# A sandwich layer on one core: norm, transposes and q, k, v products of blocks 1 and 2 made one block ahead, in two homes

## The reference

```python
h = layernorm(x); xc = silu(causal_conv4(h))                 # along the tokens
q, k = l2norm(h @ Wq), l2norm(h @ Wk)                        # per head, 16 heads of 16
v = layernorm(h @ Wv)                                        # per head
i, gamma = sigmoid(xc @ Wig + big), sigmoid(xc @ Wg + bg)
mem[t] = gamma[t] * mem[t-1] + i[t] * k[t] * v[t]            # a scan along the tokens
out = groupnorm(layernorm(mem) * q) * sigmoid(xc @ Wog + bog)
h = x0 + out @ Wo;  y = h + (silu(ln(h) @ Wgate) * (ln(h) @ Wval)) @ Wout    # FF = 1024
```

## Time and profile before

| | us |
|---|---|
| median of 3 runs (569.54 to 570.79) | 569.62 |
| profiled execution, whole | 570.92 |
| its span, first to last instruction | 569.2 |
| TensorE busy, products of `BUSY` among it | 529.4 |
| products of `BUSY` (L887), 254 records | 33.1 |
| VectorE busy | 387.9 |
| ScalarE busy | 267.5 |
| GpSimd busy | 108.1 |

### The profile page before, as it was taken

How to read it: one execution, slowest core, us unless ns; L and a number is a source line. 1 busy time by engine, 2 the same in 40 slices (tenths; PEclk the granted TensorE clock), 3 DMA queues, 4 the chain that set the end, 5 groups by cost and what they waited for, 6 DMA issues and landing times.

```text
span 569.2 us, 8506 instructions
## 1 busy us (share of the span) xinstructions
PE 529.4 (93%) x2646; PEld 424.9 (75%) x2646; DVE 387.9 (68%) x1165; ACT 267.5 (47%) x489; POOL 108.1 (19%) x133
## 2 busy tenths in 40 slices
PE   7989889997799999999999997999996899999983
PEld 6568655876567777876687885888875799999872
DVE  5998847788756889853976962515567666767547
ACT  4943755154654243576414337111344456666605
POOL 1500041000033320004041000050014024444500
PEclk9999899999799999999999999999999999999997
DMA  8951000010200020120010001020139224444284
GB/s 282 419 200 38 2 0 0 1 37 1 74 1 0 30 85 1 37 74 1 1 47 28 31 9 37 1 75 1 38 85 284 86 78 131 124 130 132 79 294 158
DMA packets 29631, 44.56 MB, mean 78 GB/s; under 512 B 3164, under 2 KB 24284, under 8 KB 29244
## 3 DMA queue, kind: packets, MB, share of 16 engines
q1 hardware_dynamic: 24595, 33.07, 18.3%
q0 software_dynamic: 3408, 9.38, 4.5%
q10 hardware_dynamic: 1584, 1.57, 0.9%
HBM read 27.67 MB, written 16.34 MB: 77 GB/s over the span
## 4 chain that ended last, share of the span: by engine, by line
PE 72%; DVE 14%; ACT 6%; DMA 4%; issue 2%; SPq 0%; POOL 0%; DVEq 0%; POOLq 0%; ACTq 0%
PE psum L868 15%; PE psum L827 12%; PE psum L828 12%; PE psum L829 12%; PE psum L909 6%; PE psum L933 3%; DMA RDNR<-rdn 2%; PE psum L887 2%; PE psum L968 2%; PE psum L837 2%; PE psum L929 2%; PE psum L1047 1%; PE psum L1064 1%; DVE XC L1403 1%; DMA YF<-y_routed 1%
## 5 line engine op out<-in xcount | busy, mean ns | idle before, releaser
L729 ACT ACTIVATE SM<-psum 128x512 f32<-128x512 f32 (+1 forms) x56 | 33.1, 594 | 118.5 <-PE psum L829 89.0
L1578 DVE TENSOR_TENSOR SM<-SM,psum 128x512 f32<-128x512 f32 (+1 forms) x56 | 38.3, 683 | 54.3 <-ACT SM L729 50.3
L593 POOL DMA_INDIRECT x_dispatched<-XN,dest x32 | 33.2, 1038 | 155.9 <-DVE XN L1646 147.4
L868 PE MATMUL psum<-WOU,SM 128*128 128x256 f32 x256 | 60.4, 380 | 0.0
L868 PEld LDWEIGHTS psum<-WOU,SM 128*128 128x128 f32 x256 | 48.0, 189 | 10.1 <-issue 1.9
L584 POOL TENSOR_TENSOR QKV<-QKV,hvec 128x256 f32<-128x256 f32 x16 | 12.3, 771 | 206.3 <-ACT IG L665 178.0
L602 POOL DMA_INDIRECT y_routed<-GO,g_dest x39 | 37.6, 965 | 68.1 <-ACT GO L799 67.8
L909 PE MATMUL psum<-WQKV,HT 128*128 128x512 f32 (+1 forms) x128 | 46.2, 509 | 3.6 <-ACT QKV L658 1.9
L868 PE MATMUL psum<-SDN,SM 128*128 128x256 f32 (+1 forms) x192 | 44.6, 381 | 0.0
L909 PEld LDWEIGHTS psum<-WQKV,HT 128*128 128x128 f32 x128 | 24.8, 199 | 23.8 <-issue 18.9
L868 PEld LDWEIGHTS psum<-SDN,SM 128*128 128x128 f32 (+1 forms) x192 | 35.8, 189 | 6.6 <-issue 1.3
(11 more groups left out here) (325 smaller groups left out, 1295.6 us busy)
## 6 DMA issues: line engine op xcount, KB each, us to landing
XG<-x_dispatched SPq DMA_DIRECT2D x39, 130.0 KB
YF<-y_routed SPq DMA_DIRECT2D x8, 512.0 KB, 7.1
RUPR<-rup SPq DMA_DIRECT2D x1, 2816.0 KB
X<-x SPq DMA_DIRECT2D x4, 512.0 KB, 6.4
x_after_attention<-X SPq DMA_DIRECT2D x4, 512.0 KB, 2.8
...
```

The lines of the kernel that those rows point to most:

```text
L593: nc.gpsimd.indirect_dma_start(XD[:, :], bass.IndirectOffsetOnAxis(dest[:, i, old + j:old + j + 1], 0), XN[:, j, :], None).then_inc(dispat ...
L729: nc.scalar.activation(SM[0:rows, g % 3, 0:tb], p_pair(n)[0][0:rows, 0:tb], ACT.Silu).then_inc(silu_ready, 1)
L868: last = nc.tensor.matmul(p_down[:, j // 2, (j % 2) * D:(j % 2 + 1) * D], SM[0:rows, g % 3, j * P:(j + 1) * P], weight[0:rows, m, :], star ...
L1578: nc.vector.tensor_tensor(SM[0:rows, g % 3, 0:tb], SM[0:rows, g % 3, 0:tb], value_rows(n, rows)[:, 0:tb], ALU.mult).then_inc(hid_ready, 1)
```

## The change

- A second home `QKV1` stands beside `QKV`; block b uses home b % 2 (`qkv(b)`). It lies where the squares of block 0 lay; these move into room that is free then.
- Block 1's rows are not fetched: `ln0` reads them from `X[:, 1]`, which is loaded anyway, and whose load is issued right behind the gate weights, ahead of Wo, Wgate, Wval and Wout.
- `q` is now only products and copy; squares, sums and GpSimd's scaling are a step of their own, `sq`.
- `ht`, `q` of block 1 stand behind `mt` of block 0 on TensorE, `ht`, `q` of block 2 among the last steps of block 1, ahead of its `h2` (`_rows`). Both blocks use banks 2 to 5 for q, k, v in turns of two (`q_banks`) and `p_down` for the transposes (`ht_banks`). New waits on TensorE keep these banks apart: `ht` of block 1 waits for block 0's scan, that of block 2 for `mlp_read`; `og` and `wo` of block 0 wait until the copies of block 1's q, k, v are through.
- On VectorE, `ln0` of block 1 moves from behind block 0's `norm` 1 to ahead of its first `sq`; `split` 1 from behind `h2` 1 to ahead of `sq` 2. The root of the first half of block 0's k and v is a Sqrt on ScalarE and a reciprocal in place of eight steps on VectorE.
- `BUSY` falls from 127 products to 42; none stands any more ahead of `og`, `ht` 2, `xt` 0 and the second `h2`.
- The tables of `PLACE` and `FIRST` are new for all blocks.

```diff
+    early = [s for s in rows[1] if s[0] == "q"]
+    at = rows[0].index(("ht", 2, 0)) + 1
+    rows[0][at:at] = early
...
 FIRST = {
     "pe": """
-        ht:0 q:0 q:1 q:2 q:3 g:0 g:1 g:2 ut:0a ut:0b mt:0a mt:0b og:0a og:0b wo:0a wo:0b ht:+0 h2:0a h2:0b q:+0 q:+1
-        q:+2 mup:0 q:+3 mup:1""",
+        ht:0 q:0 q:1 q:2 q:3 g:0 g:1 g:2 ut:0a ut:0b mt:0a mt:0b ht:+0 q:+0 q:+1 q:+2 q:+3 og:0a og:0b wo:0a wo:0b
+        h2:0a h2:0b mup:0 mup:1""",
...
 BUSY = {
-    ("ht", 0, 0, 0): 26, ("ut", 0, 0, 0): 9, ("mt", 0, 0, 1): 10, ("og", 0, 0, 0): 46, ("og", 0, 0, 1): 16, ("h2", 0, 0, 0): 8,
-    ("ht", 2, 0, 0): 4, ("xt", 0, 0, 0): 6, ("h2", 1, 0, 0): 2,
+    ("ht", 0, 0, 0): 18, ("ut", 0, 0, 0): 10, ("mt", 0, 0, 0): 8, ("h2", 0, 0, 0): 6,
 }
...
         def q_banks(b, m):
+            if b in (1, 2):
+                return psum[:, 2 + 2 * (m % 2):4 + 2 * (m % 2), :]
             return psum[:, 2 * m:2 * m + 2, :] if b == 0 else p_main
...
+        def qkv(b):
+            return (QKV0, QKV1)[b % 2]
+        def normed_from(b, j):
+            return X[:, 1, j, :] if b == 1 else qkv(b)[:, j, 0:D]
+        def ht_banks(b):
+            return p_down if b in (1, 2) else p_main
...
             sp.dma_start(GW[:, :, D:2 * D], rows(wog)).then_inc(w_in["gw"], 16)
+            load_x(1)
             sp.dma_start(WO[:, :, :], rows(wo)).then_inc(w_in["wo"], 16)
...
             load_x(0)
-            load_x(1)
...
# ScalarE
-                if stage == "fetch" and b > 0:
-                    act.wait_ge(affined, prior)
+                if stage == "fetch" and b > 1:
+                    act.wait_ge(affined, PSTART[b - 1])
...
+                if stage == "rs" and u == 0 and m == 1:
+                    both = slice(0, 2 * len(mine) * HEADS)
+                    act.wait_ge(var_done["rs"], 1)
+                    nc.scalar.activation(rs[:, both], va[:, both], ACT.Sqrt).then_inc(root_ready["rs"], 1)
...
# TensorE
+                    if stage == "og":
+                        pe.wait_ge(qkv_copied, START[2] - 1)
...
                 if (stage, m) == ("ht", 0):
                     if b == 1:
-                        pe.wait_ge(normed, prior)
-                    if b > 1:
+                        pe.wait_ge(mem_ready, C * prior)
+                    if b == 2:
+                        pe.wait_ge(mlp_read, 1)
+                    if b > 2:
                         pe.wait_ge(hr_ready, prior)
-                    to_features(p_main, lambda j: QKV[:, j, 0:D], nj, hn_ready, old).then_inc(ht_psum, 1)
+                    to_features(ht_banks(b), lambda j: qkv(b)[:, j, 0:D], nj, hn_ready, old).then_inc(ht_psum, 1)
...
                 if stage == "wo":
                     if b == 0:
                         pe.wait_ge(w_in["wo"], 16)
+                        pe.wait_ge(qkv_copied, START[2])
...
# VectorE
+                    elif u == 0:
+                        dve.wait_ge(root_ready["rs"], 1)
+                        pairs = y.rearrange("p (j h) -> p j h", j=len(mine))
+                        nc.vector.reciprocal(rr[:, t0:t1, HEADS:], pairs).then_inc(rr_ready, 1)
```

122 lines of the change are left out of this document (75 added, 47 removed), and 48 rows, old and new, of the table PLACE.

## The result

| | before | after |
|---|---|---|
| median of 4 runs each on one chip | 570.20 (569.54 to 571.14) | 563.84 (562.82 to 564.56) |
| profiled execution, its span | 570.92, 569.2 | 562.82, 561.0 |
| mean granted clock of TensorE | 0.983 | 0.971 |

What follows compares the result with a forecast made beforehand. TensorE's work was taken to bound the kernel outside two holes where it waits for VectorE. Terms -7.5 and -6.6 gave -14.1 on the profiled 570.9, so 556.8, median 555.5; range 549 to 564 for 8 in 10.

Steps and rivals of the forecast that it cites:

- q products in the holes cost nothing: TensorE's waits in block 0's attention and between blocks 0 and 1: q products moved there are free at full clock.
- `norm` 1 ends at 57.9: Block 0's start on VectorE: net 2.9 us later, so `norm` 1 ends at 57.9 instead of 55.0.
- 14.4 us from `norm` 1 to H2L: Block 0: H2L 14.4 us after `norm` 1 instead of 18.1, ending at 72.3, when the first `mup` starts.
- 17.8 from there to `ut`: From H2L at 72.3, 10.1 us to the root and 7.7 to `u`'s end; block 1's `ut` at 90.1.
- first term: Gain at block 1's `ut` from its q products in the first hole: -7.5 us, bounds -10.3 and -3.
- After the hole 7.95 are gone: Behind the second hole, three of block 2's q products leave TensorE's path: 2.79 + 2.58 + 2.58 = 7.95 us.
- 1.3 for ScalarE's copies: Second hole: block 2's last q copy and XN stand ahead of `ln2` on ScalarE, costing 1.3 us.
- Second term: Gain from block 2's q products in the second hole: -7.95 + 1.3 = -6.6 us, bounds -10 and -2.
- The rest 0: From block 2's `ut` on, nearly the same order and path as before: 0 us, within -1 and +2.
- The clock as it is: The sum leaves the number of TensorE clock falls on the path unchanged; each costs about 1.6 us.
- one of the holes is not free: Rival: queued copies delay `h2` and `xt`, or the start is 4 us later; one term shrinks to a third; 560.5, chance 0.12.
- The signs named beforehand: Right: block 1's `ut` near 90 after about 2 us waiting for VectorE; wrong: `og` after 60, q products of 4.2.

Runs made afterwards that it cites:

- q1nb: Changed kernel with block 1's q products back behind `h2` and 46 `BUSY` products ahead of `og`, without the 16 between its halves; 574.18 us, ratio 1.0058.
- q2late: Changed kernel with block 2's q products, copies and squares back behind `route`, and the second hole's 4 + 6 + 2 `BUSY` products back; 572.14 us, ratio 1.0033.
- rootdve: Changed kernel with the first k, v root back on VectorE in eight steps instead of ScalarE's root and a reciprocal; 566.34 us, ratio 0.9905.
- nrut: Changed kernel with first-half `nr` ahead of second-half `mt`, first-half `norm` ahead of second-half `var`, and no ten `BUSY` products ahead of `ut`; 562.05 us, ratio 0.9852.
- last: Changed kernel with XC's silu ahead of the root, Wval's low part later, xtearly's order, and 16 + 5 `BUSY` products near 338 us; 560.91 us, ratio 0.9825.
- xtearly: Changed kernel with only the second hole reordered: `xt` ahead of block 2's last q product or copy, `route` behind `h2`'s transposes; 561.20 us, ratio 0.9821.
- xsfirst: Changed kernel with XC's silu on ScalarE moved ahead of the k, v root and Wval's split; 562.28 us, ratio 0.9838.
- warm2: Changed kernel with `BUSY` products added in the second hole: 5 ahead of block 1's `h2`, 8 ahead of block 0's `route`; 563.40 us, ratio 0.9865.
- warm1: Changed kernel with `BUSY` products added in block 0: 9 ahead of the second half's `h2`, 12 ahead of the first `mup`; 564.48 us, ratio 0.9901.
- five: Changed kernel with the edits of xsfirst, nrut and xtearly together, and Wval's low part behind `og`'s product with GA; 562.47 us, ratio 0.9857.

## Why the prediction was wrong, step by step

- *q products in the holes cost nothing*: right. 10.59 us in each, no gap. Their places are worth 8.5 us (first `mup`, q1nb) and 8.3 us (`ut` of block 2, q2late, with `BUSY` back). Alone neither would pay for the rest of the change: q1nb and q2late are both slower than before.
- *`norm` 1 ends at 57.9*: **the step that failed**, the 2.9 us by which VectorE's start was to be later. It ended at 60.7, 5.7 later than before. Of the 2.8 that were left out, 1.3 lie in VectorE's own work, 1.0 in its wait for TensorE's `ut`, and 0.5 between the scan and `norm` 1.
  - VectorE's work to the end of `u` is 4.2 later, not 2.9, although the convolution began 1.0 earlier. Taking out eight root steps for a reciprocal was counted at 3.3 and gave 1.3 (rootdve): the steps were long because GpSimd was at work beside them, and that stretch stays and falls on the rows that come in their place. `ln0` took 5.1 instead of 3.8, with three of its small steps stretched by 1.3 in all (the 2 us more that the prediction named beside the sum and left out), and Wval's low part 2.8 instead of 2.35.
  - TensorE's side had no term at all. XC's silu, on which the gates wait, now stands behind Wval's split and the root's wait on ScalarE: gates 3.4 us later, and 1.7 longer at the low clock. Wval's split costs ScalarE 1.9 us there, the root 0.9. With ten `BUSY` products behind the gates, `ut` came 0.96 after VectorE was ready for it; nrut takes that wait away.
  - In `last` `norm` 1 ends at 57.8, the first `mup` is at 73.11 and `ut` of block 1 at 90.97; forecast were 57.9, 72.3 and 90.1. This is no proof of the forecast: `last` has Wval's low part taken out of the start, 2.35 us that the forecast had counted in.
- *14.4 us from `norm` 1 to H2L*: right, 60.7 to 75.0. *17.8 from there to `ut`*: 18.1. So the first term came out at -4.4 instead of -7.5, nearly all of it from the step above.
- *After the hole 7.95 are gone*: right, 32.4 us from `mup` of block 1 to `ut` of block 2 became 24.5. *1.3 for ScalarE's copies*: 1.0 at HN (17.30 against 16.33), so nearly right. Not in the sum was the place of `xt` and `route`, some 1.8 us (xtearly). From sum to `mup` were 24.9 us, with a q product of 3.49 at the low clock among them, and are 27.6 in the profiled execution, 25.9 at the full clock. Second term -5.4 instead of -6.6 in the profiled execution; in nrut, xsfirst, rootdve and warm2, whose clock stayed up there, it is -7.1. So what is missing from this term is the clock of one execution. That -7.1 is so near to -6.6 is partly luck: the order of `xt` and `route` was not in the sum, and neither was what the first q product, which stood ahead of `mup`, gave.
- *The rest 0*: 1.3 us are lost at `mt` of block 2 (8.45 ahead instead of 9.8), where TensorE waits 1.24 for the scan; no run tests why. In all 8.1 us between the two profiled executions. The medians say 6.4: the changed kernel's profiled execution is its fastest, the one before is not, and the prediction's own step from trace to median (1.3) went the other way.
- *The clock as it is*: more of TensorE's time ran at 1.2 GHz (0.971 against 0.983 of the whole, some 10 us in one piece from 71 to 81). warm1 shows that this piece cost 0.6 at `ut` of block 1 and no time that the runs can tell; the piece from 149 to 156 cost 1.7 in the trace, as the forecast's 1.6 for a fall. The Trainium skill, "TensorE: Matmul & The Clock Gate", section "Why this matters for your kernels", advises against idle gaps; the clock did fall behind several of them, as it says, and adding `BUSY` gave no gain that the runs can tell in any kernel here. In the traces it pays at one place, the ten products ahead of `ut` once the gates are early (`last` against `five`, 2.0 us at `og`).
- The rival "one of the holes is not free" was nearest in time (560.5). Of its two mechanisms the copies in the queue cost the 1.0 us above; the other, a later start, is what happened, by 2.8 us instead of 4.
- The signs named beforehand did their work: `og` after 60 was to mean wrong, and it began at 60.25. `ut` of block 1 waited 0.31 for VectorE instead of about 2.
- One reading of the rows was off: the low slices of TensorE's row between the blocks end at 157, not 170. Nothing in the sum uses it.
